# Self-attention scores: from a maximum and a scaling copy to a negated product and a running minimum

## The chip, the cores and the metric

The kernel runs on one core of a Trainium2 chip. The metric is the device time of one execution in microseconds (us). Its parts are called here PE (TensorE, with PEld for its weight loads), DVE (VectorE), ACT (ScalarE), POOL (GpSimd) and SP (SyncE, which starts nearly all DMAs).

## The reference

The input x is 4 x 1024 x 512 (batch, positions, features). A first layer attends from x to a context of 64 positions with 16 heads, with a bias of 4 x 16 x 1024 x 64, and a layer norm. The second layer is a block of self-attention, cross-attention to the same context, and a gated feed-forward part (512 to 2 x 2048, exact Gelu, 2048 to 512). The change is in the self-attention, whose q, k and v are rounded to 8 bits with the step sizes dq, dk and dv:

```python
sim  = einsum('bhid,bhjd->bhij', fq(q, dq), fq(k, dk)) * SCALE   # 16 heads, 1024 x 1024 scores each, head size 32
attn = softmax(sim, axis=-1)
out  = einsum('bhij,bhjd->bhid', fq(attn, dw), fq(v, dv))        # attn is rounded to steps of 1/255
```

In the kernel q and k are whole numbers, so the score is one product times a positive factor, `scale` = dq * dk * SCALE, and the softmax of a row is exp(scale * s - scale * max s) over its sum.

## The kernel before

The 4096 positions are cut into 8 chunks of 512, two per batch entry. The program is one list per engine, written out by hand; the engines meet at semaphores only, and each works through its own list in order. For a batch entry come the first layers of both chunks (`cross`), and then for each chunk `self_attention` and `middle` (the output product, the cross-attention and its norms). The feed-forward part of a chunk isn't a stage of its own: `feed` puts its pieces into slots of later stages ("hosted"), 18 or 28 of 48 steps of four products each into the slots of the next chunk's self-attention. The first chunk's self-attention has nothing hosted.

`self_attention(n)` has 64 units per chunk, 512 in all: a unit is one head and 128 queries against 1024 keys. Slot s of the loop holds, on each engine:

- PE: the scores of unit s, two matmuls into two banks of PSUM (L2008, L2009); two such pairs of banks take turns, so the scores of unit s wait until the exponential of unit s - 2 has released its pair. Then hosted products; then, five units behind, eight transposes of the weights (L2020) into bank 4, and for every fourth unit the product with v (L2034).
- DVE: the maximum of each row of unit s (`mx1`, L1612); the evacuation of the transposes of unit s - 5 from bank 4 (`w1T`, L1624), without which PE can't transpose the next unit; hosted instructions (`gate`, L1523, and `x`, L1486).
- ACT: a copy of the maximum times -scale into `nb1` (L1296), and the exponential of the 1024 scores, with `nb1` as its bias and `scale` as its factor, and with the row's sum from the accumulator (L1302). Hosted: `gate` (L1235), a Gelu over four tiles (L1241) with a table load ahead of it and another ahead of the next exponential, and `u_hi` (L1227).
- POOL: two units behind, for each pair of units the step times the sum (`den1`, L991) and its inverse (`rec1`, L993), and for each unit the division with an added half step (`w1b`, L998).

Of the kernel before, what the change touches and what calls it, by code (L numbers as in the profile page):

```python
# [34 lines left out]
Q_LOW, Q_HIGH = -128.0, 127.0  # L35
W_HIGH = 255.0


# [221 lines left out]
def build(nc, a, out):  # L260

    ctx = ExitStack()
    with ctx:
# [48 lines left out]
        rr = [sb(f"row_scale{i}", [P, H]) for i in range(NT)]  # L312
        mx1 = sb("mx1", [P, 4])
        nb1 = sb("nb1", [P, 4])
# [138 lines left out]
        units = [(n, u) for n in chunks for u in range(UNITS)]  # L453
        maxed1 = signal("maxed1", units)
        nb_ready = signal("nb_ready", units)
# [630 lines left out]
        def _(act):  # L1086
# [204 lines left out]
            def self_attention(n):  # L1291

                for s in range(S_SLOTS):
                    if s < UNITS:
                        act.wait_ge(maxed1.sem, maxed1.at((n, s)))
                        act.activation(nb1[:, s % 4:s % 4 + 1], mx1[:, s % 4:s % 4 + 1], ACT.Copy,  # L1296
                                       scale=nscale[:, 0:1]).then_inc(nb_ready.sem, 1)
                        act.wait_ge(nb_ready.sem, nb_ready.at((n, s)))
                        if s >= NE:
                            act.wait_ge(w1_ready.sem, w1_ready.at((n, s - NE)))  # L1300
                        i = bank_of(("s1", n, s))
                        act.activation(e1[s % NE][:], psum[:, i:i + 2, :].rearrange("p i n -> p (i n)"), ACT.Exp,  # L1302
                                       bias=nb1[:, s % 4:s % 4 + 1], scale=scale[:, 0:1],
                                       accum_out=sum1[:, s % 8:s % 8 + 1]).then_inc(emptied[i], 1)
                    hg, at = divmod(s - LAG_T - 18, 16)
                    if hg >= 0 and at == 0:
                        weighted_high(n, hg)
                    if n >= 1:
                        feed(n - 1, host_plan(n - 1), first_in_S(n) + s)
                weighted_high(n, HG - 1)  # L1310
# [47 lines left out]
        def _(dve):  # L1358
# [247 lines left out]
            def self_attention(n):  # L1606

                for s in range(S_SLOTS):
                    if s < UNITS:
                        wait_filled(dve, ("s1", n, s))  # L1610
                        i = bank_of(("s1", n, s))
                        dve.tensor_reduce(mx1[:, s % 4:s % 4 + 1], psum[:, i:i + 2, :].rearrange("p i n -> p (i n)"),  # L1612
                                          AX, ALU.max).then_inc(maxed1.sem, 1)
                    u = s - LAG_T
# [534 lines left out]
```

## Time and profile before

| what | us |
|---|---|
| median of 3 runs | 3404.15 |
| the runs | 3402.14 to 3405.04 |
| span of the profiled execution | 3406.4 |
| busy: PE, PEld | 2956.5, 2148.8 |
| busy: DVE, POOL, ACT | 2099.8, 1772.2, 1669.4 |

The profiled execution is one execution by itself, and its span of 3406.4 us is the time from its first instruction to its last. Busy times are sums over the span. A chain of waits is followed back from the last instruction: at each step to what released it, or to the instruction ahead of it on its engine; "issue" in it is time in which nothing shown was waited for. PE's granted clock is given as a share of 2.4 GHz (0.5 is 1.2 GHz).

### The profile page before, as it was taken

The page shows a single profiled execution, that of the slowest core. Times are in us where ns is not written, and L with a number is a line of the kernel's source. Part 1 is how long each engine was busy: PE and PEld are TensorE (multiplying, and loading weights), DVE is VectorE, ACT ScalarE, POOL GpSimd, SP SyncE. Part 2 cuts the span into 40 slices and gives each one's busy share as a digit, 9 for nine tenths or more (in the row PEclk, how much of TensorE's full clock was granted, in tenths as well). Part 3 has the DMA queues.
Part 4 walks back from the last instruction along what each step waited for, and adds up shares of the span by engine and source line. Part 5 has one row for each costly group of instructions (what it writes and reads, how often), then busy time and mean ns, then how long its engine had stood idle before and what let it go on. Part 6 is the DMA issues. An engine that isn't in the chain of part 4 may idle for free.

```text
span 3406.4 us, 50798 instructions
## 1 busy us (share of the span) xinstructions
PE 2956.5 (87%) x19712; PEld 2148.8 (63%) x19712; DVE 2099.8 (62%) x3031; ACT 1669.4 (49%) x2690; POOL 1772.2 (52%) x1695
## 2 busy tenths in 40 slices
PE   7677686887899899799889899899988889889999
PEld 6555455556677657566667656656777646656777
DVE  4556585773666586685565586676565577677521
ACT  5332572873333475574333375475333276386321
POOL 3554573884545274575355185475365176376321
PEclk9888657898999899899999999899999989999999
DMA  8753103334443213324353313323353322232444
GB/s 276 220 200 133 56 1 133 108 119 179 162 164 141 91 63 125 130 88 155 130 176 111 123 51 141 126 74 135 133 188 99 142 75 100 97 120 75 171 152 160
DMA packets 199758, 436.40 MB, mean 128 GB/s; under 512 B 94944, under 2 KB 103392, under 8 KB 182368
## 3 DMA queue, kind: packets, MB, share of 16 engines
q1 hardware_dynamic: 199520, 433.15, 36.1%
q8 instruction: 158, 2.59, 0.3%
q14 instruction: 80, 0.66, 0.1%
HBM read 363.38 MB, written 65.54 MB: 126 GB/s over the span
## 4 chain that ended last, share of the span: by engine, by line
PE 60%; DVE 11%; POOL 11%; ACT 7%; issue 6%; DMA 2%; SPq 1%; POOLq 0%; DVEq 0%; ACTq 0%
PE psum L1724 17%; PE psum L1726 15%; PE psum L1725 15%; PE psum L2020 5%; POOL w1b L998 3%; PE psum L2008 3%; DVE mx L1612 2%; ACT e L1302 2%; PE psum L2034 2%; ACT psum L1189 1%; DVE w1T L1624 1%; POOL u_lo L1017 1%; POOL rec L993 1%; DMA fw_lo<-pieces 1%; POOL w_lo L901 1%
## 5 line engine op out<-in xcount | busy, mean ns | idle before, releaser
L1612 DVE TENSOR_REDUCE mx<-psum 128x1 f32<-128x1024 f32 x512 | 623.1, 1218 | 121.2 <-PE psum L2009 121.0
L998 POOL TENSOR_SCALAR w1b<-e,rec 128x1024 f16<-128x1024 f32 x512 | 574.7, 1122 | 138.6 <-PE psum L2020 66.3
L1302 ACT ACTIVATE e<-psum,nb,scale 128x1024 f32<-128x1024 f32 x512 | 617.5, 1206 | 19.8 <-POOL w1b L998 3.1
L1724 PE MATMUL psum<-h_hi,fw_hi 128*128 128x512 f32 x1024 | 464.9, 454 | 30.9 <-DVE h_lo L1388 10.0
L1624 DVE TENSOR_SCALAR w1T<-psum 128x1024 bf16<-128x1024 f16 x512 | 352.0, 687 | 176.4 <-PE psum L2020 163.6
L1725 PE MATMUL psum<-h_lo,fw_hi 128*128 128x512 f32 x1024 | 415.8, 406 | 0.0
L1726 PE MATMUL psum<-h_hi,fw_lo 128*128 128x512 f32 x1024 | 415.2, 405 | 0.0
L2020 PEld LDWEIGHTS psum<-ident,w1b 128*128 128x128 f16 x4096 | 260.7, 105 | 207.7 <-issue 127.7
L2020 PE MATMUL psum<-ident,w1b 128*128 128x128 f16 x4096 | 354.3, 236 | 40.2 <-DVE w1T L1624 21.1
L907 POOL TENSOR_TENSOR rstd<-ve,mhalf 128x1 f32<-128x1 f32 x128 | 86.8, 678 | 484.8 <-DVE ve L1494 484.8
L1724 PEld LDWEIGHTS psum<-h_hi,fw_hi 128*128 128x128 f32 x1024 | 199.6, 195 | 152.4 <-issue 99.4
L1486 DVE TENSOR_TENSOR x<-psum,x 128x512 f32<-128x512 f32 x224 | 152.3, 685 | 232.4 <-PE psum L1726 231.6
L1724 PE MATMUL psum<-w_hi,ht_hi 128*128 128x512 f32 x640 | 257.5, 402 | 20.2 <-DVE e L1549 13.7
L1017 POOL TENSOR_TENSOR u_lo<-gate,u_hi 128x512 fp32r<-128x512 f32 x128 | 164.7, 1289 | 202.6 <-ACT u_hi L1227 196.8
L1296 ACT ACTIVATE nb<-mx,nscale 128x1 f32<-128x1 f32 x512 | 149.6, 292 | 235.6 <-DVE mx L1612 227.1
L901 POOL TENSOR_TENSOR w_lo<-mixed,w_hi 128x512 fp32r<-128x512 f32 x140 | 189.5, 1376 | 132.0 <-ACT w_hi L1196 132.0
L1724 PE MATMUL psum<-fw_hi,u_hi 128*128 128x512 f32 x512 | 226.2, 442 | 31.2 <-POOL u_lo L1017 13.7
L1725 PE MATMUL psum<-w_lo,ht_hi 128*128 128x512 f32 x640 | 251.7, 393 | 0.0
L1726 PE MATMUL psum<-w_hi,ht_lo 128*128 128x512 f32 x640 | 251.3, 393 | 0.0
L1726 PEld LDWEIGHTS psum<-h_hi,fw_lo 128*128 128x128 f32 x1024 | 200.8, 196 | 47.2
L1134 ACT ACTIVATE qt<-psum,rounder,inv 128x512 f32<-128x512 f32 x128 | 99.9, 780 | 248.1 <-PE psum L1726 244.6
L2009 PE MATMUL psum<-k_odd,q_turned 32*128 32x512 bf16 x512 | 220.1, 431 | 0.0
(181 smaller groups left out, 6237.0 us busy)
## 6 DMA issues: line engine op xcount, KB each, us to landing
fw_hi<-pieces SPq DMA_DIRECT2D x168, 512.0 KB, 3.3
fw_lo<-pieces SPq DMA_DIRECT2D x168, 512.0 KB, 4.4
w_hi<-kept SPq DMA_DIRECT2D x45, 1024.0 KB, 4.9
w_lo<-kept SPq DMA_DIRECT2D x45, 1024.0 KB, 7.4
mixed<-mixed SPq DMA_DIRECT2D x32, 1024.0 KB, 5.4
fbias<-in_fside_Bx16xSxS SPq DMA_DIRECT2D x64, 256.0 KB, 3.2
unsplit<-in_L_xattn_ff_w SPq DMA_DIRECT2D x24, 512.0 KB, 5.1
pieces<-fw_hi SPq DMA_DIRECT2D x24, 512.0 KB, 2.7
```

Source lines behind the costliest of these rows:

```text
L901: pool.tensor_tensor(w_lo[s][:, k, :], w_mixed[s][:, k, :], w_hi[s][:, k, :].bitcast(F32), ALU.subtract).then_inc(block_lo_done.sem, 1)
L998: pool.tensor_scalar(w1b[u % NH][:], e1[u % NE][:], rec1[:, u % 8:u % 8 + 1], HALF, ALU.mult, ALU.add).then_inc(w1_ready.sem, 1)
L1017: pool.tensor_tensor(u_lo[:, m, :], gate[:, m, :], u_hi[:, m, :].bitcast(F32), ALU.subtract).then_inc(u_lo_done.sem, 1)
L1302: act.activation(e1[s % NE][:], psum[:, i:i + 2, :].rearrange("p i n -> p (i n)"), ACT.Exp, bias=nb1[:, s % 4:s % 4 + 1], scale=scale[:, 0:1],
L1486: return emptied_bank(dve.tensor_tensor(xt, bank(bank_of(key)), xt, ALU.add), key)
L1612: dve.tensor_reduce(mx1[:, s % 4:s % 4 + 1], psum[:, i:i + 2, :].rearrange("p i n -> p (i n)"), AX, ALU.max).then_inc(maxed1.sem, 1)
L1624: emptied_bank(dve.tensor_scalar(w1T[u % 8][:].rearrange("p k q -> p (k q)"), bank(bank_of(key)).bitcast(FP16), -HALF, W_HIGH, ALU.add, AL ...
L1724: pe.matmul(o, s_hi, m_hi, start=first, stop=False)
L1725: pe.matmul(o, s_hi, m_lo, start=False, stop=False)
L1726: return pe.matmul(o, s_lo, m_hi, start=False, stop=last)
L2009: ins = pe.matmul(bank(i + 1), q1_turned[turned, hg, t * P:t * P + P], k1[1][turned, hg, :], start=True, stop=True)
L2020: ins = pe.transpose(bank(bank_of(key)).bitcast(FP16)[:, k * P:k * P + P], w1b[u % NH][:, k * P:k * P + P], ident16[:])
```

## The change

DVE's maximum becomes one instruction that multiplies the 128 x 1024 scores by -scale and writes them back to where they stood in PSUM; its second operation is a minimum with a number above all scores, which leaves the products as they are and makes the accumulator output the row's minimum, that is -scale * max. That output goes straight to `nb1`. ACT's copy goes, with the semaphore `maxed1` and the tile `mx1`. The exponential takes the immediate factor -1.0 in place of the column `scale`: exp(-1.0 * (-scale * s) + nb1). The product on the scores was inside the exponential before; now it is made on DVE and rounded once.

```diff
+LARGEST = 3.0e38
...
-        maxed1 = signal("maxed1", units)
         nb_ready = signal("nb_ready", units)
...  (ScalarE)
                     if s < UNITS:
-                        act.wait_ge(maxed1.sem, maxed1.at((n, s)))
-                        act.activation(nb1[:, s % 4:s % 4 + 1], mx1[:, s % 4:s % 4 + 1], ACT.Copy,
-                                       scale=nscale[:, 0:1]).then_inc(nb_ready.sem, 1)
                         act.wait_ge(nb_ready.sem, nb_ready.at((n, s)))
...
                         act.activation(e1[s % NE][:], psum[:, i:i + 2, :].rearrange("p i n -> p (i n)"), ACT.Exp,
-                                       bias=nb1[:, s % 4:s % 4 + 1], scale=scale[:, 0:1],
+                                       bias=nb1[:, s % 4:s % 4 + 1], scale=-1.0,
                                        accum_out=sum1[:, s % 8:s % 8 + 1]).then_inc(emptied[i], 1)
...  (VectorE)
-                        dve.tensor_reduce(mx1[:, s % 4:s % 4 + 1], psum[:, i:i + 2, :].rearrange("p i n -> p (i n)"),
-                                          AX, ALU.max).then_inc(maxed1.sem, 1)
+                        scores = psum[:, i:i + 2, :].rearrange("p i n -> p (i n)")
+                        dve.tensor_scalar(scores, scores, nscale[:, 0:1], LARGEST, ALU.mult, ALU.min,
+                                          accum_out=nb1[:, s % 4:s % 4 + 1]).then_inc(nb_ready.sem, 1)
```

ScalarE at the first hosted Gelus in the second chunk's self-attention, before (`e_0` to `e_4` are the exponentials' five buffers, `nb_ready` and `maxed1` the semaphores of the bias and of the maximum):

```order
L1302 ACTIVATE e_0,sum<-psum,nb,scale 128x1024 [waits w1_ready,nb_ready]
L1235 ACTIVATE gate<-psum,col_L_xattn_ff_b 128x512 [waits u_lo_done,filled7]
L1241 ACT_TABLE_LOAD [waits emptied7]
L1241 ACTIVATE gate<-gate 128x2048 [waits emptied6]
L1296 ACTIVATE nb<-mx,nscale 128x1 [waits maxed1]
L1302 ACT_TABLE_LOAD [waits w1_ready]
L1302 ACTIVATE e_1,sum<-psum,nb,scale 128x1024 [waits nb_ready]
L1214 ACTIVATE fw_hi<-unsplit 128x1024 [waits raw_piece_loaded0]
L1296 ACTIVATE nb<-mx,nscale 128x1 [waits maxed1]
```

and now:

```order
L1298 ACTIVATE e_0,sum<-psum,nb 128x1024 [waits w1_ready,nb_ready]
L1234 ACTIVATE gate<-psum,col_L_xattn_ff_b 128x512 [waits u_lo_done,filled7]
L1240 ACT_TABLE_LOAD [waits emptied7]
L1240 ACTIVATE gate<-gate 128x2048 [waits emptied6]
L1298 ACT_TABLE_LOAD [waits w1_ready]
L1298 ACTIVATE e_1,sum<-psum,nb 128x1024 [waits nb_ready]
L1213 ACTIVATE fw_hi<-unsplit 128x1024 [waits raw_piece_loaded0]
L1298 ACTIVATE e_2,sum<-psum,nb 128x1024 [waits w1_ready,nb_ready]
```

The copy ahead of each exponential is gone, and behind the Gelu the table load comes at once, without a wait for the maximum.

VectorE in the same stretch, at a hosted `gate`, before (`filled0`, `filled2` and `filled4` are PE's signals for the banks):

```order
L1612 TENSOR_REDUCE mx<-psum 128x1 [waits filled2]
L1624 TENSOR_SCALAR w1T<-psum 128x1024 [waits filled4]
L1523 SCALAR_TENSOR_TENSOR gate<-psum,col_L_xattn_ff_b,gate 128x512 [waits filled6,gelu_done]
L1612 TENSOR_REDUCE mx<-psum 128x1 [waits filled0]
L1624 TENSOR_SCALAR w1T<-psum 128x1024 [waits filled4]
```

and now:

```order
L1609 TENSOR_SCALAR psum,nb<-psum,nscale 128x1024 [waits filled2]
L1621 TENSOR_SCALAR w1T<-psum 128x1024 [waits filled4]
L1519 SCALAR_TENSOR_TENSOR gate<-psum,col_L_xattn_ff_b,gate 128x512 [waits filled6,gelu_done]
L1609 TENSOR_SCALAR psum,nb<-psum,nscale 128x1024 [waits filled0]
L1621 TENSOR_SCALAR w1T<-psum 128x1024 [waits filled4]
```

The order stays; the first kind of instruction now writes 128 x 1024 back to PSUM and the bias beside it.

## Rows read from the trace of the kernel before

**Rows 1.** Self-attention: start:end, length, busy PE, PEld, DVE, ACT, POOL, clock, DMA, GB/s.

```profile
377.00:512.00 135.00, 110.64 (x1080) 63.09 (x1077) 116.65 (x128) 104.58 (x198) 107.43 (x129) 0.51 0.03 13
600.00:768.00 168.00, 147.16 (x1328) 93.72 (x1326) 121.25 (x137) 132.22 (x230) 138.08 (x140) 0.92 0.33 114
1162.00:1304.00 142.00, 129.83 (x1244) 76.41 (x1243) 120.55 (x137) 113.85 (x212) 111.31 (x130) 0.90 0.19 69
1413.00:1571.00 158.00, 144.04 (x1333) 92.94 (x1331) 122.03 (x138) 125.83 (x224) 112.20 (x129) 0.95 0.31 113
1943.00:2085.00 142.00, 127.84 (x1246) 75.40 (x1246) 121.52 (x139) 114.42 (x213) 111.46 (x130) 0.93 0.20 72
2195.00:2352.00 157.00, 143.26 (x1331) 92.28 (x1329) 121.34 (x137) 124.58 (x221) 112.21 (x129) 0.95 0.32 113
2726.00:2871.00 145.00, 131.19 (x1249) 76.85 (x1247) 121.68 (x139) 114.83 (x213) 111.50 (x130) 0.91 0.20 71
2980.00:3140.00 160.00, 145.85 (x1339) 94.09 (x1339) 123.10 (x139) 127.54 (x228) 113.94 (x132) 0.95 0.30 105
sum 1207.00, PE 1079.82 PEld 664.79 DVE 968.12 ACT 957.86 POOL 918.13; mean PE 134.98 PEld 83.10 DVE 121.01 ACT 119.73 POOL 114.77
```

**Rows 2.** The chain of waits over the whole run, by line.

```profile
by line: PE psum L1724 17.4%; PE psum L1726 15.2%; PE psum L1725 15.2%; issue 6.0%; PE psum L2020 5.0%; POOL w1b L998 3.2%; PE psum L2008 2.9%; DVE mx L1612 2.0%; ACT e L1302 1.6%; PE psum L2034 1.6%; ACT psum L1189 1.5%; DVE w1T L1624 1.3%
```

**Rows 3.** The chain in pieces (start us, us, what): first and last copy.

```profile
378.70 0.30 ACT nb L1296
...
3135.07 0.18 ACT nb L1296
```

**Rows 4.** Groups of instructions by line: count, busy us, mean ns, idle before.

```profile
L1612 DVE TENSOR_REDUCE mx<-psum 128x1 f32<-128x1024 f32 x512 | 623.1, 1218 | 121.2 <-PE psum L2009 121.0
...
L1624 DVE TENSOR_SCALAR w1T<-psum 128x1024 bf16<-128x1024 f16 x512 | 352.0, 687 | 176.4 <-PE psum L2020 163.6
...
L1296 ACT ACTIVATE nb<-mx,nscale 128x1 f32<-128x1 f32 x512 | 149.6, 292 | 235.6 <-DVE mx L1612 227.1
...
L1302 ACT ACTIVATION_READ_ACCUMULATOR e<-psum,nb,scale 128x1 f32 x512 | 97.7, 191 | 0.0
```

**Rows 5.** Instructions in time, stretch 1: start us, us, engine, line.

```profile
438.54 1.23 DVE L1612 TENSOR_REDUCE mx<-psum 128x1 f32<-128x1024 f32 x1 [0.40 <-PE psum L2009]
...
439.80 0.29 ACT L1296 ACTIVATE nb<-mx,nscale 128x1 f32<-128x1 f32 x1 [0.76 <-DVE mx L1612]
...
440.13 1.21 ACT L1302 ACTIVATE e<-psum,nb,scale 128x1024 f32<-128x1024 f32 x1
```

**Rows 6.** The chain in pieces behind a Gelu in stretch 4.

```profile
1441.00 1.91 ACT gate L1241
1442.91 0.18 ACT nb L1296
...
1444.41 1.30 ACT e L1302 x2
```

**Rows 7.** Groups by line: other PSUM instructions.

```profile
L1188 ACT ACTIVATE ht_hi<-psum,unit_v 128x512 fp32r<-128x512 f32 x64 | 43.6, 682 | 130.8 <-PE psum L2097 73.0 <-PE psum L2034 57.9
...
L1189 ACT ACTIVATE psum<-psum,unit_v 128x512 f32<-128x512 f32 x64 | 41.9, 655 | 0.0
...
L1661 DVE TENSOR_TENSOR e<-psum,row_max 128x1024 f32<-128x1024 f32 x32 | 39.2, 1224 | 1.1
```

**Rows 8.** VectorE in time: a 128x1 instruction and the next.

```profile
905.96 0.15 DVE L1494 TENSOR_SCALAR ve<-mv 128x1 f32<-128x1 f32 x1
906.03 0.54 DVE L1505 TENSOR_SCALAR z<-x,mv,rstd 128x512 f32<-128x512 f32 x1
```

**Rows 9.** The chain in pieces, stretch 1, four units apart.

```profile
440.60 1.23 DVE mx L1612
...
448.64 1.23 DVE mx L1612
```

**Rows 10.** The chain of waits in stretch 3, by line.

```profile
by line: POOL w1b L998 16.0%; issue 10.9%; PE psum L2020 9.9%; PE psum L1724 8.9%; PE psum L2008 7.1%; POOL rec L993 6.1%; POOL u_lo L1017 5.4%; PE psum L1725 4.9%; PE psum L1726 4.9%; DVE mx L1612 4.2%; ACT e L1302 3.8%; DVE w1T L1624 3.4%
```

More of the change, by code:

```diff
@@ L312, in build @@
         rr = [sb(f"row_scale{i}", [P, H]) for i in range(NT)]
-        mx1 = sb("mx1", [P, 4])
         nb1 = sb("nb1", [P, 4])
```

## The prediction

> **What bounds the kernel now.** I read three views in this order: busy time per stretch, the chain of waits that ended last, and single instructions in time. The changed lines run only in self-attention, 512 units (a unit is one head of one block of 128 queries against all 1024 keys) in eight stretches of 64. All eight are in [rows 1], 1207 us in all: the third, fifth and seventh are alike (142, 142, 145 us), and so are the fourth, sixth and eighth (158, 157, 160 us). In none of them is one engine full. Stretch 1 has nothing hosted in it and runs at a granted clock of 0.51: VectorE is busy for 116.7 of 135 us, PE for 110.6. Stretch 2 hosts the splits of the feed-forward weights, and GpSimd is the fullest but for PE. Stretches of the third kind have PE at 129.8, VectorE at 120.6 and GpSimd at 111.3 of 142 us; those of the fourth kind are PE's (144.0 of 158).
>
> So it is the chain that says what an edit is worth. Over the whole run it holds 2.0% of the max reduction (L1612) and 1.6% of the exponential (L1302) [rows 2]. Read piece by piece through the eight stretches it holds 60 pieces of the max and 60 of the little ScalarE copy (L1296), 15.6 us of the copy in all; its first and its last piece stand in [rows 3]. By stretch the copy is there 5, 11, 5, 9, 6, 10, 5 and 9 times, the max 19, 7, 6, 5, 7, 5, 6 and 5 times. 36 of the 60 copies directly follow a max (a piece of about 0.30 us). 24 follow work of ScalarE itself (about 0.18 us, as in the last piece of [rows 3], since the rest overlaps what is ahead). And of the 60 maxima 24 aren't followed by the copy at all: there the chain goes on to VectorE's next instruction, the evacuation w1T (L1624), for which PE waits.
>
> **The change part by part.** *Removed on ScalarE:* 512 copies of 292 ns, 149.6 us busy [rows 4]. ScalarE is idle before them for 235.6 us, so most of that is time it would wait anyway; what counts is the latency. In time [rows 5]: the max ends at 438.54 + 1.23 = 439.77, the copy starts at 439.80, the exponential at 440.13. From the end of the max to the start of the exponential is 0.36 us, and 0.33 of this goes (copy and one hand-over). In the chain that is 15.6 us of copies and 60 hand-overs of 0.02, 16.8 us. Behind a Gelu the chain reads Gelu, copy, table load, exponential [rows 6]: the Gelu of 1.91 us ends at 1442.91, the copy's own piece is 0.18, and the exponential starts at 1444.41. The table load isn't removed; it moves up by the copy.
>
> *Replaced on VectorE:* the max over 128x1024 in PSUM, 1218 ns [rows 4], becomes a multiply in place over the same 128x1024 with a running minimum. No row shows VectorE writing fp32 to PSUM, nor one of its instructions with an accumulator output, so I bound both. The read of 1024 fp32 from PSUM with all 1024 written, to SBUF, takes 1224 ns (L1661) [rows 7]: 6 ns more than the max. On ScalarE the same 128x512 takes 682 ns to SBUF and 655 ns in place in PSUM [rows 7], so in place is no slower there. The lowest cost is then -0.03 us (the difference of these two); the highest is one pass more over the 1024 elements, by the max's own 1.22 us, should reading and writing one bank alternate. I take +0.02, next to the 6 ns row.
>
> The accumulator read: ScalarE shows one behind each exponential, 191 ns [rows 4]. On VectorE the nearest row is the 128x1 instruction ve, 0.15 us, and the next one on the engine starts 0.07 us after it [rows 8]. So the read holds the queue for 0.07 to 0.19 us, and if the profile folds it into the main instruction, for 0. I take 0.07 for the queue and for the signal alike. The new instruction is then longer than the max by d = 0.09 us, bounds -0.03 and 1.41.
>
> The Trainium skill speaks against the change here. "VectorE: DVE Perf Modes", section "Two Vector instructions with no wait between them", says an instruction that writes out its accumulator is two, and the page's sections on DRAIN and on rules for authors say that each instruction pays a flush and a fixed part (about 150 cycles, 0.16 us by the page's clock), so that it's the count that matters. By that, and calling it an estimate from the page, d would be about 0.18 and the chain would give back 5 us more than in my sum. The 0.07 us between ve and the next instruction [rows 8] does not agree with a full fixed part each time; no run here yet shows it for an accumulator.
>
> *What is queued behind it:* w1T (687 ns [rows 4]) stands behind each max. In stretch 1 the chain runs max, w1T, eight transposes, w1T, ... and the same place returns 448.64 - 440.60 = 8.04 us later, four units on, with one max in the chain per round [rows 9]. There the copy isn't on the path, and d is paid. In the third kind of stretch GpSimd's w1b is 16.0% of the chain and the max 4.2% [rows 10]; the first is not touched.
>
> *The sum.* The 24 copies behind ScalarE's own work: nothing else could be in time there, since VectorE has long finished its max and waits as well; they count in full, 24 x 0.20 = 4.8 us gained. The 36 behind a max: 36 x (0.32 - 0.09) = 8.3 us, of which I take two thirds, 5.5: a third is kept back because PE, VectorE and GpSimd are each over 78% busy in stretches of the third kind [rows 1] and another path is due soon behind the shortened one, but 28 of the 60 copies stand in the fourth kind, where VectorE and GpSimd have over 20% left. The 24 maxima ahead of w1T: 24 x 0.09 = 2.2 us lost. Together -8.1, say -8 us. The profiled execution has a span of 3406.4 us, 2.2 above the median of 3404.15; it goes to about 3398, and the median to 3396. The chain of before, edited, is still a path afterwards: with all 16.8 us gone and d = 0 it bounds the gain, 3387 as a median, as long as durations and PE's clock stay.
>
> ScalarE's immediate scale of -1.0 in place of a column costs nothing that a row shows. Semaphores: one hand-over fewer, no new wait; bank order and buffers are as before.
>
> **The rivals.**
> *The chain closes up.* The exponential is earlier, but PE's next scores stand in its queue behind transposes that wait for w1b from GpSimd. For it: w1b's share [rows 10], and PE 144.0 of 158 in the fourth kind [rows 1]. Against it: the stalls at a Gelu, where all wait for ScalarE [rows 6]. Only those 4.8 us stay, less the 60 x 0.09 = 5.4: no change, 3404, or up to 5 us less.
>
> *VectorE becomes the bound (slower).* Its queue alternates the new instruction and w1T; a round of four units needs 4 x (1.218 + 0.687) = 7.62 of 8.04 us in stretch 1 [rows 4, 9]. It decides there from d = 0.42 / 4 = 0.105 us, and in the third kind from (142 - 120.6) / 64 = 0.33 us, with some of it sooner. At d = 0.3: stretch 1 grows by 16 x (0.3 - 0.105) x 4 = 12.5 us, the 41 maxima in the chain elsewhere by 12.3, and in the third kind about 2 us each are added where w1T comes late, 6 us; less the 12 us or so that the copy gives back, +19: 3423. The full extra pass (1.41) would make VectorE 64 x 3.32 = 212 us a stretch, near 3404 + 512 x 1.0 = 3900; nothing in the rows points there. For this rival: two unseen features in one instruction, and the skill's rule above, which with 0.18 would put stretch 1 just past the point (+5 us), about 3404 in all. Against it: the 6 ns and the 655 ns of [rows 7].
>
> *All of the copy's time comes back.* The paths behind are slack enough and the table load, which now does not wait for a maximum, starts at once: -16.8 + 5.4 = -11.4, 3393. For it: in the fourth kind 28 of 60 copies stand in the chain. Against it: the busy shares.
>
> **How the numbers follow.** Most of the chain's saving, 3396: 0.44. All of it, 3393: 0.16. The chain closes up, 3399 to 3404: 0.20. VectorE bound: 0.20, of which 0.03 lie below 3411, 0.13 up to 3425 and 0.04 above. A measurement of this kernel can tell about 0.2%, 6.8 us, from no change. Faster by more than this means below 3397.3: six tenths of the first case, which spreads over 3392 to 3400, and the second whole, and 0.03 for a PE clock that holds its upper level a little longer: 0.45. Slower: 0.13 + 0.04 = 0.17. Within 0.2% is the rest, 0.38. The range leaves out 0.2: from 3388, the chain's floor, to 3418, d a little under 0.3. The likeliest case alone: 3391 to 3401.
>
> **What would show it.** VectorE's new group: a main part of 1.22 to 1.26 us and an accumulator read under 0.2; above 1.35 together the forecast is wrong. ScalarE: no L1296; from the end of VectorE's read to the start of the exponential some 0.03 us. In the chain the exponential directly behind VectorE or a table load. Stretch 1 unchanged within 2 us, each of the fourth kind 1 to 3 us shorter. If stretch 1 grows by 5 or more, VectorE has become the bound.

## The result

The changed kernel takes 3385.4 us (median of 4 runs, 3383.1 to 3391.6); the kernel before 3404.6 beside it. The ratio is 0.9949, 95% interval 0.9932 to 0.9966: 17 us less, by the medians 19. The forecast was 3396, with a range from 3388, so the time lies 3 us below the range: the direction was right, and the gain twice the 8 us that I gave it. The profiled execution has a span of 3381.5 us.

Busy time over the span (page of the changed kernel, part 1):

```profile
PE 2951.5 (87%) x19712; PEld 2148.1 (64%) x19712; DVE 2134.1 (63%) x3543; ACT 1484.3 (44%) x2178; POOL 1772.7 (52%) x1695
```

ScalarE has lost 185 us against the kernel before. The copies were 149.6 of it and the exponentials are shorter by 46.6 in sum (the two come to more than 185, since records overlap a little); VectorE has gained 34. The groups by line answer to [rows 4]. The exponential before:

```profile
L1302 ACT ACTIVATE e<-psum,nb,scale 128x1024 f32<-128x1024 f32 x512 | 617.5, 1206 | 19.8 <-POOL w1b L998 3.1
```

and the changed kernel:

```profile
L1609 DVE TENSOR_SCALAR_CACHE_REDUCE psum<-psum,nscale 128x1024 f32<-128x1024 f32 x512 | 657.5, 1286 | 98.7 <-PE psum L2006 98.7
...
L1298 ACT ACTIVATE e<-psum,nb 128x1024 f32<-128x1024 f32 x512 | 570.9, 1115 | 412.4 <-DVE psum L1609 398.2 <-POOL w1b L997 11.3
...
L1621 DVE TENSOR_SCALAR w1T<-psum 128x1024 bf16<-128x1024 f16 x512 | 352.7, 689 | 137.0 <-PE psum L2017 135.3
...
L1609 DVE DVE_READ_ACCUMULATOR psum<-psum,nscale 128x1 f32 x512 | 72.4, 141 | 0.0
```

L1609 is the new VectorE instruction: 1286 ns for the max's 1218, and its accumulator read is a record of its own, 141 ns. L1298 is the exponential: 1115 ns for 1206. That is the first thing the prediction did not have. In time, at the place of [rows 5]:

```profile
439.54 1.29 DVE L1609 TENSOR_SCALAR_CACHE_REDUCE psum<-psum,nscale 128x1024 f32<-128x1024 f32 x1 [0.16 <-PE psum L2006]
...
440.75 0.14 DVE L1609 DVE_READ_ACCUMULATOR psum<-psum,nscale 128x1 f32 x1
440.75 0.69 DVE L1621 TENSOR_SCALAR w1T<-psum 128x1024 bf16<-128x1024 f16 x1
440.92 1.11 ACT L1298 ACTIVATE e<-psum,nb 128x1024 f32<-128x1024 f32 x1 [0.85 <-DVE psum L1609]
```

The next w1T starts 1.21 us after the start of the new instruction, as early as the accumulator read itself; it was 1.15 us after the start of the max before. Over the stretches, where VectorE goes from one to the other without a wait, the distance was 1.13 or 1.14 us in more than half of the cases before and is 1.20 or 1.21 in more than half of them now. So in VectorE's queue the new instruction mostly costs 0.07 us more, and the accumulator read nothing on top. From the start of the max to the start of the exponential it was 440.13 - 438.54 = 1.59 us; it is 440.92 - 439.54 = 1.38 now. My sum had 1.59 - 0.33 + 0.09 = 1.35. Of the signs that I gave, the main part (1.286 us, I said 1.22 to 1.26) missed; main part and read are 1.43 us as a sum of their two records, over the 1.35 that I named, but from the start of one to the end of the other it is 1.35, since they overlap. From the end of the read to the exponential it is 0.03 us, as forecast, and stretch 1 is unchanged (130.2 and 130.0 us below).

The stretches with 0, 18 and 28 hosted steps (columns as in [rows 1]):

```profile
376.00:507.00 131.00, 108.81 (x1048) 61.92 (x1048) 119.43 (x190) 79.37 (x133) 104.55 (x125) 0.50 0.04 14
...
1154.00:1290.00 136.00, 124.99 (x1244) 74.23 (x1242) 123.33 (x199) 90.00 (x147) 111.15 (x129) 0.94 0.20 73
1401.00:1557.00 156.00, 144.03 (x1334) 92.81 (x1333) 128.53 (x202) 103.31 (x162) 113.90 (x132) 0.95 0.30 112
```

and the chain of waits over the whole run, to be read beside [rows 2]:

```profile
by line: PE psum L1721 17.3%; PE psum L1723 15.2%; PE psum L1722 15.2%; issue 7.0%; DVE psum L1609 5.1%; PE psum L2017 4.3%; PE psum L2005 2.7%; POOL w1b L997 2.4%; DVE w1T L1621 2.2%; PE psum L2031 1.5%; ACT psum L1188 1.4%; POOL w_lo L900
```

and in stretch 3, beside [rows 10]:

```profile
by line: DVE psum L1609 30.9%; issue 12.7%; DVE w1T L1621 12.7%; POOL w1b L997 10.5%; POOL rec L992 4.2%; POOL u_lo L1016 3.8%; PE psum L1721 3.6%; POOL x L912 3.4%; PE psum L2005 2.9%; PE psum L1722 2.1%; PE psum L1723 2.1%; PE psum L2017 
```

The max and the exponential had 2.0% and 1.6% of the whole chain. VectorE's instruction now has 5.1%, the exponential is no longer among the first. In stretch 3 GpSimd's w1b fell from 16.0 to 10.5%, and VectorE rose from 4.2 to 30.9%, w1T behind it from 3.4 to 12.7%: VectorE, busy for 123.3 of 136 us, has become the largest part of that stretch's chain, and the stretch is still shorter than before. In stretch 4 the chain still is PE's.

The lengths of the stretches, from the first start of VectorE's max (or new) instruction to its last end, from one profiled execution each, in us (a few us between two rows may be the execution's own: the runs of the kernel before range from 3392 to 3410, and the profiled execution of the kernel before was 13 us longer than that of immediate_only, where the medians differ by 4):

| kernel | 1 | 2 | 3 | 4 | 5 | 6 | 7 | 8 | sum |
|---|---|---|---|---|---|---|---|---|---|
| before | 130.2 | 171.2 | 141.7 | 157.8 | 139.6 | 158.2 | 141.7 | 157.8 | 1198 |
| changed | 130.0 | 165.0 | 135.8 | 155.9 | 138.6 | 156.3 | 137.8 | 156.9 | 1176 |
| column_scale | 130.3 | 165.5 | 138.0 | 157.2 | 138.6 | 156.9 | 136.9 | 158.0 | 1181 |
| immediate_only | 130.0 | 167.3 | 137.3 | 158.0 | 137.5 | 158.0 | 137.2 | 158.0 | 1183 |
| copy_kept | 130.8 | 170.7 | 139.1 | 158.1 | 138.0 | 158.5 | 138.3 | 158.6 | 1192 |
| vector_only | 131.8 | 168.5 | 139.0 | 159.0 | 143.0 | 159.0 | 139.2 | 159.1 | 1199 |
| to_sbuf | 130.8 | 157.7 | 132.3 | 139.5 | 132.6 | 139.6 | 132.1 | 141.8 | 1106 |
| den_on_act | 130.0 | 149.9 | 128.6 | 139.8 | 130.9 | 139.7 | 128.6 | 139.8 | 1087 |

22 of the 25 us between the two profiled spans lie in the stretches, most of it in 2, 3 and 7. The experiments named in the other rows are told below.

### The profile page after: what moved, and what is told of

Its sections match the earlier page's. It is cut to its first block, busy times and chain, and to the rows that moved or that the text cites. A ratio compares the mean times of both kernels' runs of the same rounds, so it can differ in the third digit from the quotient of the medians.

```text
span 3381.5 us, 50798 instructions
## 1 busy us (share of the span) xinstructions
PE 2951.5 (87%) x19712; PEld 2148.1 (64%) x19712; DVE 2134.1 (63%) x3543; ACT 1484.3 (44%) x2178; POOL 1772.7 (52%) x1695
## 4 chain that ended last, share of the span: by engine, by line
PE 59%; DVE 16%; POOL 9%; issue 7%; ACT 5%; DMA 2%; SPq 1%; POOLq 0%; DVEq 0%; ACTq 0%
PE psum L1721 17%; PE psum L1723 15%; PE psum L1722 15%; DVE psum L1609 5%; PE psum L2017 4%; PE psum L2005 3%; POOL w1b L997 2%; DVE w1T L1621 2%; PE psum L2031 1%; ACT psum L1188 1%; POOL w_lo L900 1%; POOL u_lo L1016 1%; POOL rec L992 1%; ACT ht_hi L1187 1%; DMA fw_lo<-pieces 1%
## 5 line engine op out<-in xcount | busy, mean ns | idle before, releaser
L1298 ACT ACTIVATE e<-psum,nb 128x1024 f32<-128x1024 f32 x512 | 570.9, 1115 | 412.4 <-DVE psum L1609 398.2
L1609 DVE TENSOR_SCALAR_CACHE_REDUCE psum<-psum,nscale 128x1024 f32<-128x1024 f32 x512 | 657.5, 1286 | 98.7 <-PE psum L2006 98.7
L900 POOL TENSOR_TENSOR w_lo<-mixed,w_hi 128x512 fp32r<-128x512 f32 x140 | 191.9, 1394 | 130.9 <-ACT w_hi L1195 130.9
L1722 PEld LDWEIGHTS psum<-h_lo,fw_hi 128*128 128x128 f32 x1024 | 201.8, 197 | 25.9
L1722 PE MATMUL psum<-fw_lo,u_hi 128*128 128x512 f32 x512 | 209.3, 409 | 0.0
```

The costliest lines, as they stand in the source:

```text
L900: pool.tensor_tensor(w_lo[s][:, k, :], w_mixed[s][:, k, :], w_hi[s][:, k, :].bitcast(F32), ALU.subtract).then_inc(block_lo_done.sem, 1)
L1609: dve.tensor_scalar(scores, scores, nscale[:, 0:1], LARGEST, ALU.mult, ALU.min, accum_out=nb1[:, s % 4:s % 4 + 1]).then_inc(nb_ready.sem, 1)
L1722: pe.matmul(o, s_hi, m_lo, start=False, stop=False)
```

## The experiments

All ratios below are against the kernel before on the same chip, with their 95% intervals; 0.001 is 3.4 us. A difference of two ratios has an interval wider than either: 5 to 7 us each way against the changed kernel, whose own is 6. The first four part the change in three: VectorE's instruction, ScalarE's copy, and the exponential's factor.

**column_scale**: the changed kernel with the factor from a column.

```diff
-                                       bias=nb1[:, s % 4:s % 4 + 1], scale=-1.0,
+                                       bias=nb1[:, s % 4:s % 4 + 1], scale=mone[:, 0:1],
```

> The changed kernel, but the exponential's factor of -1.0 comes from a 128x1 column in place of an immediate; nothing else differs. Theory A (the operand): the 91 ns that the exponential lost (1206 to 1115) belong to the immediate; here it takes about 1206 again, and since these 91 ns lie in the chain and ahead of GpSimd's work too, about half of the gain of 19 us goes: 3394. Rival B (the neighbour): the exponential is shorter because no ScalarE copy is issued right ahead of it, or because VectorE has just written the bank; it stays at 1115 here, and the time at 3385.

3388.5 us, 0.9965 (0.9953 to 0.9976): the immediate is worth 0.0016, 5 us, of the change, which this pair alone does not tell from nothing; immediate_only does. The group of the exponential:

```profile
L1298 ACT ACTIVATE e<-psum,nb,mone 128x1024 f32<-128x1024 f32 x512 | 616.7, 1205 | 376.1 <-DVE psum L1609 362.8 <-POOL w1b L997 11.5
```

1205 ns: the duration follows the operand, not the neighbour.

**immediate_only**: the kernel before with the factor as an immediate.

```diff
-                                       bias=nb1[:, s % 4:s % 4 + 1], scale=scale[:, 0:1],
+                                       bias=nb1[:, s % 4:s % 4 + 1], scale=0.02 * 0.02 * DH ** -0.5,
```

> The kernel before, with maximum and copy as they were; only the exponential's factor is an immediate, the product of the step sizes of these inputs (0.02 * 0.02 / sqrt(32)), in place of the column. Theory A: the exponential at about 1115 ns, and the time near 3395, 9 us below the kernel before. Rival B: 1206 ns and 3404.

3397.0 us, 0.9987 (0.9978 to 0.9996), 4 us less:

```profile
L1302 ACT ACTIVATE e<-psum,nb 128x1024 f32<-128x1024 f32 x512 | 570.8, 1115 | 23.0 <-POOL w1b L998 6.7
```

1115 ns with max and copy in place. Theory A holds for the duration; for the time it was too generous (4 to 5 us, not 9).

**copy_kept**: the changed kernel, with a copy between VectorE's minimum and the bias.

```diff
+                        act.wait_ge(mined1.sem, mined1.at((n, s)))
+                        act.activation(nb1[:, s % 4:s % 4 + 1], mn1[:, s % 4:s % 4 + 1], ACT.Copy,
+                                       scale=pone[:, 0:1]).then_inc(nb_ready.sem, 1)
                         act.wait_ge(nb_ready.sem, nb_ready.at((n, s)))
...
-                                          accum_out=nb1[:, s % 4:s % 4 + 1]).then_inc(nb_ready.sem, 1)
+                                          accum_out=mn1[:, s % 4:s % 4 + 1]).then_inc(mined1.sem, 1)
```

> The changed kernel, but VectorE's minimum goes to a tile of its own and ScalarE copies it (times a column of ones) into the bias, as it copied the maximum before; the immediate -1.0 stays. Theory A: exponential 1115 ns, VectorE's instruction 1286 and its read as in the changed kernel. The copy's latency comes back: 0.33 us in the chain wherever the exponential follows VectorE or a Gelu, so about 10 us over the changed kernel: 3396 to 3400. Rival B (the copy is what shortens the exponential, and what the change is worth): 1206 ns, and at least 3404.

3400.3 us, 0.9999 (0.9991 to 1.0008): 17 us over the changed kernel. The exponential takes 1115 ns here too. It was the copy that the change lived on, and it costs more than the 10 us that I expected. Its chain of waits still holds 61 pieces of the copy, as that of the kernel before held 60, and in the stretches 3, 5 and 7 it already holds some 40 pieces of VectorE's new instruction each, as many as the changed kernel's.

**vector_only**: copy_kept with the column of -1.0 as the exponential's factor, so that of the change only VectorE's longer instruction is left.

```diff
-                                       bias=nb1[:, s % 4:s % 4 + 1], scale=-1.0,
+                                       bias=nb1[:, s % 4:s % 4 + 1], scale=mone[:, 0:1],
```

> As copy_kept, and the exponential's factor is a column of -1.0: of the change only VectorE's longer instruction (1286 ns for 1218, and the accumulator read) is left. If d = 0.13 us is paid by the chain of before alone (60 maxima), 8 us slower than the kernel before: 3412. If VectorE becomes the bound in the stretches without much hosted work, 12 to 20 us slower: 3417 to 3425. If it is hidden behind GpSimd and PE: 3404 to 3407.

3406.1 us, 1.0018 (1.0009 to 1.0027), 6 us slower than the kernel before on that chip (3401.3), with an interval of 3 to 9: it lies between the 8 us that the chain of before pays by itself and the 3 at most of an instruction that is hidden, and far from a VectorE that bounds all. From here the copy goes (to column_scale, -0.0053, 18 us) and then the column (to the changed kernel, -0.0016). The three parts are +6, -18 and -5 us, -17 in all. The other order gives the same within the intervals: immediate_only -4, from it to copy_kept +4, and from there to the changed kernel -17.

**copy_twice**: the kernel before with one more ScalarE copy ahead of the real one.

```diff
+                        act.activation(pad1[:, s % 4:s % 4 + 1], mx1[:, s % 4:s % 4 + 1], ACT.Copy, scale=nscale[:, 0:1])
                         act.activation(nb1[:, s % 4:s % 4 + 1], mx1[:, s % 4:s % 4 + 1], ACT.Copy,
```

> The kernel before with a second, idle ScalarE copy of the same form ahead of the real one (into a tile that nobody reads). It lengthens by about 0.3 us what the change shortened. Theory A (the way from maximum to exponential is on the path by as much as the chain holds, and nothing is due right behind it): the mirror of the removal, which gave 17 to 18 us by the runs so far: 3418 or more, since new units come into the chain as it gets longer. Rival C (another path runs close beside it, and the removal gained by something else, as the table load that no longer waits for the maximum): under 10 us, 3403 to 3411.

3422.7 us, 1.0069 (1.0057 to 1.0081): 23 us more for one copy more, 17 to 18 us less for one less. The time answers to this latency in both directions, and not much more weakly downwards. Rival C falls.

Where the copy is felt shows in what PE waits for. Its wait for the exponential ahead of the scores, in us over the span, was in the kernel before (total, number of waits, longest)

```profile
PE psum L2008 <- ACT e L1302: 88.0, 45, 3.9
```

In total it is 83.5 in immediate_only, 92.8 in vector_only and 88.4 in copy_kept, all with the copy, and 70.5 in column_scale and 65.5 in the changed kernel, without it. So 22 to 23 us of it go with the copy in either pair.

**copy_in_hosted**: copy_kept in stretches 2, 4, 6 and 8, the changed kernel in the others.

```diff
+                        if n % 2 == 1:
+                            act.wait_ge(mined1.sem, mined1.at((n, s)))
+                            act.activation(nb1[:, s % 4:s % 4 + 1], mn1[:, s % 4:s % 4 + 1], ACT.Copy,
+                                           scale=pone[:, 0:1]).then_inc(nb_ready.sem, 1)
                         act.wait_ge(nb_ready.sem, nb_ready.at((n, s)))
...
+                                          accum_out=(mn1 if n % 2 else nb1)[:, s % 4:s % 4 + 1]
+                                          ).then_inc((mined1 if n % 2 else nb_ready).sem, 1)
```

> copy_kept cost 17 us over the changed kernel. Here ScalarE's copy is kept in the stretches 2, 4, 6 and 8 only and gone in 1, 3, 5 and 7. By the count in the chain of the kernel before, 39 of its 60 copies stand in 2, 4, 6 and 8 (11 + 9 + 10 + 9): 39 x 0.32 = 12 us over the changed kernel, 3394 to 3398 beside a kernel before of 3400. If it was a third path (VectorE and GpSimd in 3, 5 and 7) that made the removal worth more than the reading: 5 to 8 us over it, 3388 to 3392.

3392.0 us, 0.9975 (0.9964 to 0.9985): 9 us of the copy's 17 lie in the stretches 2, 4, 6 and 8, where the chain's count gives 12; the other 8 lie in 1, 3, 5 and 7, where it gives 7. It is between the two expectations. The intervals of these differences are 5 to 7 us each way, so this tells neither the two expectations apart nor how good the count is in either group.

**vector_longer**: the changed kernel with a 128x1 instruction more on VectorE.

```diff
                                           accum_out=nb1[:, s % 4:s % 4 + 1]).then_inc(nb_ready.sem, 1)
+                        dve.tensor_scalar(pad1[:, s % 4:s % 4 + 1], nscale[:, 0:1], 1.0, None, ALU.mult)
```

> The changed kernel with one more 128x1 VectorE instruction, into a tile that nobody reads, behind the accumulator read: it holds the queue for about 0.07 us more in each unit. Chain of the changed kernel: 121 of VectorE's new instructions stand in the chain in the three stretches with 18 hosted steps, 21 in the first, 19 in the others. If VectorE is now the bound there: 161 x 0.07 = 11 us more, 3397. If it only looks so, because GpSimd's chain runs level with it: under 5 us, 3386 to 3390.

3394.2 us, 0.9985 (0.9977 to 0.9994): 12 us over the changed kernel, where 11 were worked out.

```profile
L1612 DVE TENSOR_SCALAR pad<-nscale 128x1 f32<-128x1 f32 x512 | 75.9, 148 | 0.0
```

Its record is 148 ns, and what it costs is 12 / 161 = 0.075 us at each place in the chain, as ve in [rows 8] let expect. The trace shows the same without the chain: the commonest distance from the start of the new instruction to w1T went from 1.20 to 1.27 us.

```profile
439.07 0.14 DVE L1610 DVE_READ_ACCUMULATOR psum<-psum,nscale 128x1 f32 x1
439.07 0.15 DVE L1612 TENSOR_SCALAR pad<-nscale 128x1 f32<-128x1 f32 x1
439.14 0.69 DVE L1623 TENSOR_SCALAR w1T<-psum 128x1024 bf16<-128x1024 f16 x1
```

With an interval of 6 us each way, the 12 us fit a VectorE that is on the path at these places, and lie above the 5 us of one that only looks so, though not by much.

**quarter_on_act**: w1T of every fourth unit on ScalarE (without the upper clip at 255 in those units).

```diff
+                    if 0 <= u < UNITS and u % 4 == 2:      # ScalarE, behind the exponential of slot s
+                        wait_filled(act, key)
...
+                        act.activation(w1T[u % 8][:].rearrange("p k q -> p (k q)"), bank(bank_of(key)).bitcast(FP16), ACT.Copy,
+                                       bias=-HALF).then_inc(emptied[bank_of(key)], 1)
...
-                    if 0 <= u < UNITS:                     # VectorE
+                    if 0 <= u < UNITS and u % 4 != 2:
```

> The changed kernel with the evacuation w1T of every fourth unit on ScalarE, behind its exponential (without the upper clip at 255 in those units, which no weight of these inputs reaches). VectorE loses 128 x 0.69 = 88 us of work, ScalarE gains some 128 x 1.1. If VectorE's own work bounds the stretches with 18 hosted steps: up to 3 x 8 us less, 3365 to 3375. If the order of the engines matters more (PE's next transposes now wait for an exponential as well): 3385 or above.

3473.1 us, 1.0213 (1.0199 to 1.0226), 90 us slower than the changed kernel:

```profile
L1633 DVE TENSOR_SCALAR w1T<-psum 128x1024 bf16<-128x1024 f16 x384 | 264.9, 690 | 282.4 <-PE psum L2029 281.7
...
L1311 ACT ACTIVATE w1T<-psum 128x1024 bf16<-128x1024 f16 x128 | 129.8, 1014 | 50.7 <-PE psum L2029 50.7
```

VectorE has 88 us less to do and waits 282 us for PE's transposes, where it waited 135. The transposes of the next unit stand behind an evacuation that stands behind an exponential; PE waits 146 us for that evacuation:

```profile
L2029 PE MATMUL psum<-ident,w1b 128*128 128x128 f16 x4096 | 350.5, 234 | 169.1 <-ACT w1T L1311 146.1 <-POOL w1b L997 13.6 <-DVE w1T L1633 7.1
```

Taking work off the bound engine is worth nothing if the work then waits in a queue behind a slower chain.

**to_sbuf**: this comes from what the changed trace shows behind a Gelu in stretch 4 (start us, us, engine, line, idle before):

```profile
1424.69 1.28 ACT L1240 ACT_TABLE_LOAD   x1
...
1425.98 1.91 ACT L1240 ACTIVATE gate<-gate 128x2048 f32<-128x2048 f32 x1
...
1427.91 1.28 ACT L1298 ACT_TABLE_LOAD   x1
...
1429.21 1.11 ACT L1298 ACTIVATE e<-psum,nb 128x1024 f32<-128x1024 f32 x1
...
1430.47 0.39 PE L2005 MATMUL psum<-k_even,q_odd 32*128 32x512 bf16 x1 [3.34 <-ACT e L1298]
...
1430.90 1.29 DVE L1609 TENSOR_SCALAR_CACHE_REDUCE psum<-psum,nscale 128x1024 f32<-128x1024 f32 x1 [2.92 <-PE psum L2006]
```

ScalarE spends 1.28 + 1.91 + 1.28 us on two table loads and a Gelu. The scores' pair of banks is released by the exponential behind them, so PE stands for 3.34 us and then VectorE for 2.92. Since VectorE rewrites the scores anyway, it can write them to the exponential's own tile in SBUF, and release the banks itself. The wait for that tile to be free (`w1_ready`) moves from ScalarE to VectorE with it, and `nb1` has eight columns for four.

```diff
 # VectorE
+                        if s >= NE:
+                            dve.wait_ge(w1_ready.sem, w1_ready.at((n, s - NE)))
                         wait_filled(dve, ("s1", n, s))
-                        dve.tensor_scalar(scores, scores, nscale[:, 0:1], LARGEST, ALU.mult, ALU.min,
-                                          accum_out=nb1[:, s % 4:s % 4 + 1]).then_inc(nb_ready.sem, 1)
+                        emptied_bank(dve.tensor_scalar(e1[s % NE][:], scores, nscale[:, 0:1], LARGEST, ALU.mult, ALU.min,
+                                                       accum_out=nb1[:, s % 8:s % 8 + 1]), ("s1", n, s))
...
 # ScalarE
-                        act.wait_ge(nb_ready.sem, nb_ready.at((n, s)))
-                        if s >= NE:
-                            act.wait_ge(w1_ready.sem, w1_ready.at((n, s - NE)))
...
-                        act.activation(e1[s % NE][:], psum[:, i:i + 2, :].rearrange("p i n -> p (i n)"), ACT.Exp,
...
+                        wait_emptied(act, ("s1", n, s))
+                        act.activation(e1[s % NE][:], e1[s % NE][:], ACT.Exp,
...
-                                       accum_out=sum1[:, s % 8:s % 8 + 1]).then_inc(emptied[i], 1)
+                                       accum_out=sum1[:, s % 8:s % 8 + 1]).then_inc(e1_done.sem, 1)
...
 # GpSimd
-                    wait_emptied(pool, ("s1", n, u + 1))
+                    pool.wait_ge(e1_done.sem, e1_done.at((n, u + 1)))
```

> The changed kernel, but VectorE writes the scaled scores into the exponential's own SBUF tile in place of PSUM, and itself releases the pair of banks; ScalarE takes the exponential in place in SBUF. PE's next scores wait for VectorE only, no longer for ScalarE. PE waited for the exponential for 65 us in the changed kernel (and 77 us of weight loads), most of it behind the Gelus. If that wait is on the path: 15 to 25 us less, 3362 to 3372, most of it in the four stretches with 28 hosted steps. If GpSimd and VectorE bound them anyway: within 5 us of 3385. VectorE's main part: 1286 ns if the extra 68 ns over the maximum are the second operation, about 1225 if they are the write to PSUM.

3316.8 us, 0.9753 (0.9741 to 0.9766): 67 us less than the changed kernel by the ratios, where I expected 15 to 25. PE's waits ahead of the scores in the changed kernel (engine, line, waited for, us, times, longest):

```profile
PEld psum L2005 <- ACT e L1298: 77.2, 36, 3.8
...
PE psum L2005 <- ACT e L1298: 65.5, 27, 3.6
```

and in to_sbuf:

```profile
PEld psum L2004 <- DVE e L1608: 10.7, 11, 1.8
...
PE psum L2004 <- DVE e L1608: 5.5, 8, 1.3
```

In the stretches 3 and 4:

```profile
1150.00:1283.00 133.00, 122.41 (x1246) 72.91 (x1244) 123.02 (x201) 92.25 (x148) 110.94 (x130) 0.97 0.20 75
1394.00:1533.00 139.00, 137.76 (x1334) 89.26 (x1333) 124.97 (x200) 102.08 (x157) 111.95 (x129) 1.00 0.34 125
```

Stretch 4 went from 155.9 to 139.5 us by the table, with PE busy for 137.8 of 139 at a granted clock of 1.00 (0.95 in the changed kernel): the stalls went, and the granted clock rose with them; no run parts the two. Over the whole span PE is busy for 2911.1 us in place of 2951.5 for the same matmuls, so some 40 of the 72 us between the two profiled spans are PE's busy time and not its stalls. I had counted the stalls at the Gelus and neither the clock nor the waits between them. The groups:

```profile
L1608 DVE TENSOR_SCALAR_CACHE_REDUCE e<-psum,nscale 128x1024 f32<-128x1024 f32 x512 | 652.6, 1278 | 88.6 <-POOL w1b L997 51.7 <-PE psum L2005 33.3 <-issue 0.3
L1295 ACT ACTIVATE e<-e,nb 128x1024 f32<-128x1024 f32 x512 | 588.5, 1150 | 339.0 <-DVE e L1608 336.5
...
L1608 DVE DVE_READ_ACCUMULATOR e<-psum,nscale 128x1 f32 x512 | 42.2, 82 | 0.0
```

The main part is 1278 ns, so at most 8 of the 68 ns over the max are the write to PSUM; whether the rest is the second operation or the column `nscale` no run shows. The accumulator read is 82 ns for 141.

**sbuf_held**: to_sbuf with the banks released by the exponential again.

```diff
-                        emptied_bank(dve.tensor_scalar(e1[s % NE][:], scores, nscale[:, 0:1], LARGEST, ALU.mult, ALU.min,
-                                                       accum_out=nb1[:, s % 8:s % 8 + 1]), ("s1", n, s))
+                        dve.tensor_scalar(e1[s % NE][:], scores, nscale[:, 0:1], LARGEST, ALU.mult, ALU.min,
+                                          accum_out=nb1[:, s % 8:s % 8 + 1]).then_inc(nb_ready.sem, 1)
```

> As to_sbuf (VectorE writes the scaled scores to SBUF, ScalarE takes the exponential there), but the pair of banks is still released by ScalarE's exponential, as in the changed kernel. It parts the gain of to_sbuf (some 68 us over the changed kernel) in two. If it is the early release that counts (PE's next scores no longer stand behind ScalarE's Gelu): within 5 us of the changed kernel, 3382 to 3392. If it is where the data lie (a shorter accumulator read, 82 ns for 141, and another port for the exponential): 3320 to 3340.

3389.7 us, 0.9976 (0.9967 to 0.9985): the whole gain of to_sbuf is gone, and 9 us more. The exponential takes 1150 ns from SBUF, 35 more than from PSUM:

```profile
L1296 ACT ACTIVATE e<-e,nb 128x1024 f32<-128x1024 f32 x512 | 588.7, 1150 | 399.4 <-DVE e L1609 397.0
```

The two kernels differ in who releases the banks, and in no other work: it is the early release that counts.

**den_on_act**: to_sbuf with GpSimd's den on ScalarE.

```diff
+                        if s % 2 == 1:                          # ScalarE, behind the exponential
+                            at = slice(s % 8 - 1, s % 8 + 1)
+                            act.wait_ge(e1_done.sem, e1_done.at((n, s)))
+                            act.activation(den1[:, at], sum1[:, at], ACT.Copy, scale=delta[:, 3:4]).then_inc(den_ready.sem, 1)
...
-                    pool.wait_ge(e1_done.sem, e1_done.at((n, u + 1)))          # GpSimd
-                    pool.tensor_scalar(den1[:, at], sum1[:, at], delta[:, 3:4], None, ALU.mult).then_inc(den_ready.sem, 1)
```

> to_sbuf, and the product of step and sum (den, 295 ns on GpSimd for each pair of units) moves to ScalarE behind the pair's second exponential; GpSimd starts with the inverse. GpSimd's den, w1b and inverse together are 28% of to_sbuf's chain in the stretches with 18 hosted steps. If GpSimd's own work bounds those: 32 x 0.35 us, up to 8 us less in each of three, 3295 to 3305. If VectorE (20% of that chain) stands level with it: 3310 to 3317. In the stretches with 28 hosted steps PE is busy for 138 of 139 us, nothing is to be had there.

3294.7 us, 0.9690 (0.9677 to 0.9703), 21 us less than to_sbuf by the ratios, and the fastest version of this study: 3.1% under the kernel before.

```profile
L990 POOL TENSOR_TENSOR rec<-den,mone 128x2 f32<-128x2 f32 x256 | 177.0, 691 | 288.4 <-ACT den L1299 278.2
...
L1299 ACT ACTIVATE den<-sum,delta 128x2 f32<-128x2 f32 x256 | 75.6, 295 | 8.3
```

The same 295 ns are hidden on ScalarE. By the table stretches 3, 5 and 7 lost 3.7, 1.7 and 3.5 us, and stretch 2, where GpSimd also makes the low parts of the weights, 7.8; 4 and 6 nothing. So the time met the first expectation and the place did not: up to 8 us in each of 3, 5 and 7 was too much, and stretch 2, which I had left out, gave the most.

## Why the prediction was wrong in size

Two terms of the sum failed: the discount of the copies behind a max by a third, and the nothing for the immediate. My sum was -12.5 us for the copy (4.8 + 36 x 0.32 x 2/3) and +4.3 for d, -8 in all. The runs gave -18 (or -17) for the copy, +6 (or +4) for VectorE's instruction and -5 (or -4) for the immediate, -17 in all. Of the 9 us that were missing some 5 are the discount and 4 to 5 the immediate; d took one or two back.

*What bounds the kernel, and the count in the chain: right.* 60 copies with their hand-overs make 16.8 us in the chain of before; taking the copy away gave 18 us (vector_only to column_scale) and 17 (copy_kept to the changed kernel), each with an interval of 5 to 7 us each way.

*"I take two thirds, 5.5": failed.* I discounted the 36 copies behind a max for another path due soon behind them, and took 0.20 us for those behind ScalarE's own work: 12.5 us without d. The runs show 17 to 18, and PE's wait for the exponential fell by 22 to 23. No other path took the gain away, and a copy more was paid for as well (copy_twice +23 us): in the kernel before, the path from scores to exponential and back to the scores ran through PE, VectorE and ScalarE in turn, and engines at 78 to 91% of a stretch are busy in turn as well; that isn't a second path.

*"ScalarE's immediate scale ... costs nothing that a row shows": failed.* It gained 91 ns per exponential and 4 to 5 us. Every exponential on PSUM had a column as its factor, but another group of the trace of before had the price of a column. L1189 is one line of the program, the same function over 128x512 in place in PSUM, once with one column (655 ns, [rows 7]) and once with two:

```profile
L1189 ACT ACTIVATE psum<-psum,col_L_xattn_ln_b,col_L_xattn_ln_g 128x512 f32<-128x512 f32 x96 | 73.4, 764 | 0.0
```

The second column is 109 ns there, near the 91 ns of the exponential; that was a term to work out, and I put it at nothing. With the parts as measured, 3404 - 18 - 5 + 6 = 3387: the change comes to the floor that I had worked out for d = 0 (3387), because the floor held every other duration fixed. Without this term the time would have stood at the edge of the range (column_scale, 3388.5).

*d = 0.09: close.* The main part is 0.068 longer and its signal comes 0.12 us later in all (1.38 for 1.59 - 0.33 = 1.26); the queue is held for 0.07 longer where the next w1T waits for nothing, as I had it for another reason: I took 0.02 for the main part and 0.07 for the read, and it is 0.07 for the main part and nothing for the read. Alone it cost 6 us (3 to 9), where the chain's 60 x 0.09 gave 5.4.

*"The chain closes up": wrong*, by copy_twice and copy_kept. *"VectorE becomes the bound": half right.* It did, in stretches 3, 5 and 7 (some 40 pieces of its instruction in each one's chain, 6, 7 and 6 before), and with 0.07 us more in its queue, not at the 0.33 that I had worked out from the old length of the stretch. It did so in copy_kept too, which takes as long as the kernel before. So being the largest part of the chain isn't being slower. Two paths of nearly the same length would look like this; no run tests that by itself.

*Where the gain lies.* I gave the stretches of the fourth kind 1 to 3 us each, and they lost 0.9 to 1.9: right. I named no gain for the others; the third kind lost 5.9, 1.0 and 3.9, and stretch 2 lost 6.2. Part of that isn't the change: between immediate_only and before 15 us lie in the stretches, 11 of them in 3, 5 and 7, where the medians differ by 4 us in all, so most of these 15 are the two executions' own. The pairs that part the copy alone are steadier. From copy_kept to the changed kernel the stretches lost 0.8, 5.7, 3.3, 2.2, -0.6, 2.2, 0.5 and 1.7 us, 16 in all; from vector_only to column_scale 1.5, 3.0, 1.0, 1.8, 4.4, 2.1, 2.3 and 1.1, 17 in all. In either pair 5 to 6 us of the copy lie in 4, 6 and 8 together, where the 28 copies of the chain make 7 or so, and 3 to 6 in stretch 2; for the third kind the two pairs say 3 and 8.

What stays open is the share of the table load, which now comes without a wait for the maximum: it wasn't tried by itself.

## What to carry to other kernels

The chain of waits, read piece by piece and counted, gave 16.8 us for the removed latency, and two pairs of runs gave 17 and 18, within their intervals; discounting it by busy shares made it worse, so a discount needs a second chain that can be named. An operand that changes from a column to an immediate is a change of its own and wants its own bounds, from any instruction of the same engine that stands in the trace with and without it. And where an engine rewrites a PSUM tile anyway, let it write to SBUF and release the banks: that was worth about four times the change itself (67 us for 17).

## What the runs showed of the hardware

- An exponential over 128x1024 from PSUM takes 1206 ns with a column as its factor and 1115 with an immediate, bias a column in both. Over 128x512 in place in PSUM (L1189) it was 764 ns with two columns and 655 with one. From SBUF the exponential took 1150 with a column as its bias and an immediate factor, and L1335 of the kernel before 1150 with a column as its factor and none as its bias: each has one column, and what a second would cost from SBUF no run shows.
- VectorE's multiply with a running minimum over 128x1024 fp32 from PSUM: 1286 ns in place in PSUM and 1278 to SBUF (max alone 1218). Its accumulator read is 141 ns when the main part writes to PSUM and 82 when it writes to SBUF (to_sbuf and sbuf_held). The next instruction mostly started together with the read, 1.20 us after the start of the main part.
- The Trainium skill ("VectorE: DVE Perf Modes", section "Two Vector instructions with no wait between them") says that an instruction with an accumulator output is two: the trace agrees, with the 141 ns record. The fixed part of about 150 cycles, 0.16 us by the page's clock, stands in the page's section on the TRN2 errata and not in the two that I named. The record of vector_longer's 128x1 instruction, 148 ns, is near it; in the queue the instruction cost 0.07 us, and the accumulator read mostly nothing.
